# Two attention sweeps of a graph kernel: the leaky slope made by VectorE alone, from a sum in SBUF

## The reference, cut to what matters

```python
xl = (x @ Wl).reshape(n, heads, dh)
xr = (x @ Wr).reshape(n, heads, dh)
m = xl[src] + xr[dst]
e = jnp.einsum('ehd,hd->eh', jax.nn.leaky_relu(m, 0.2), att)
emax = jax.ops.segment_max(e, dst, num_segments=n)
ex = jnp.exp(e - emax[dst])
denom = jax.ops.segment_sum(ex, dst, num_segments=n)
alpha = ex / denom[dst]
out = jax.ops.segment_sum(alpha[..., None] * xl[src], dst, num_segments=n)
```

## Time and profile before

| | |
|---|---|
| median of three runs | 9611.01 us |
| the profiled execution, its own time | 9569.96 us |
| its span, first to last instruction | 9568.0 us |
| busy, share of the span | TensorE 50% (weight loads 44%), VectorE 55%, ScalarE 32%, GpSimd 49% |
| granted TensorE clock, mean | 0.685 of full |
| the 16 DMA engines, mean rate | 157 GB/s |
| from 6370 to 9474 us (the two `gatv2` sweeps with the stage between them) | VectorE busy 1784.5 of 3104.0 us, ScalarE 1025.1, GpSimd 1519.1, DMA share 0.44 |

### The profile page before, as it was taken

The page is one execution under the profiler, slowest core; times in us unless marked ns, Lnnn a source line. Parts: engine busy times, 40 slices in busy tenths (PEclk is TensorE's granted clock), DMA queues, the critical chain, the costliest instruction groups (busy, mean ns, idle before and its releaser), DMA issues. The chain is left out here.

```text
span 9568.0 us, 100223 instructions
## 1 busy us (share of the span) xinstructions
PE 4784.9 (50%) x25909; PEld 4224.4 (44%) x25909; DVE 5255.1 (55%) x9516; ACT 3094.4 (32%) x5510; POOL 4727.2 (49%) x4980
## 2 busy tenths in 40 slices
PE   2667676565555556555544434334444443444443
PEld 2656565455545355454523333333333332433332
DVE  5655555465655456555544444455555554555555
ACT  1555555222222122222222222223333332333332
POOL 4555552454554345544445555544455444454454
PEclk6565557777777777777766666666666666666665
DMA  4666553566666466666646665534444433444443
GB/s 111 173 170 175 167 166 100 170 210 198 204 196 190 141 194 210 191 189 188 187 126 177 178 180 175 173 108 127 130 133 132 125 119 110 130 133 130 129 132 101
DMA packets 1303017, 1502.46 MB, mean 157 GB/s; under 512 B 397380, under 2 KB 994787, under 8 KB 1302452
## 3 DMA queue, kind: packets, MB, share of 16 engines
q1 hardware_dynamic: 1105428, 1005.88, 34.4%
q0 software_dynamic: 197024, 490.18, 18.8%
HBM read 1070.45 MB, written 423.22 MB: 156 GB/s over the span
## 5 line engine op out<-in xcount | busy, mean ns | idle before, releaser
L778 POOL DMA_INDIRECT s_rows<-kv_tab,src_col x2346 | 2223.8, 948 | 2218.0 <-DVE s_msg L1077 1349.3
L923 PE MATMUL bank<-s_msg,s_hot 128*128 128x144 f32 (+1 forms) x9408 | 2076.8, 373 | 1620.8 <-issue 957.1
L923 PEld LDWEIGHTS bank<-s_msg,s_hot 128*128 128x128 f32 x9408 | 1748.0, 258 | 1819.8 <-issue 1098.3
L778 POOL DMA_INDIRECT s_rows<-xl_tab,src_col x1564 | 1479.3, 946 | 1513.5 <-DVE s_msg L1077 980.4
L898 PE MATMUL bank<-s_qwin,s_hot_t 128*128 128x128 f32 (+1 forms) x9408 | 1680.5, 328 | 310.7 <-issue 199.2
L818 ACT ACTIVATE s_part<-bank 128x288 f32<-128x288 f32 (+1 forms) x2352 | 895.5, 401 | 2751.2 <-remote 1590.8
L978 DVE TENSOR_TENSOR_SCAN bank<-s_neg,bank 32x128 f32<-32x128 f32 (+1 forms) x588 | 243.3, 414 | 2749.8 <-remote 2553.5
L898 PEld LDWEIGHTS bank<-s_qwin,s_hot_t 128*128 128x128 f32 x9408 | 1582.2, 252 | 301.6 <-issue 240.2
L778 POOL DMA_INDIRECT s_rows<-gat_tab,src_col x782 | 741.7, 948 | 602.3 <-DVE s_msg L1077 362.3
L812 ACT ACTIVATE s_prob<-s_diff 32x128 f32<-32x128 f32 (+1 forms) x588 | 181.0, 308 | 2517.2 <-DVE s_diff L987 1814.1
L905 PE MATMUL bank<-ident,s_seg_max 32*128 32x32 f32 (+1 forms) x588 | 166.4, 283 | 1514.7 <-ACT s_prob L812 1239.4
(11 more groups left out here) (312 smaller groups left out, 4696.2 us busy)
## 6 DMA issues: line engine op xcount, KB each, us to landing
s_qwin<-q_tab SPq DMA_DIRECT2D x3920, 64.0 KB
part_tab<-s_part SPq DMA_DIRECT2D x294, 576.0 KB
part_tab<-s_part SPq DMA_DIRECT2D x294, 544.0 KB
s_ranks<-rank_tab SPq DMA_DIRECT2D x588, 256.0 KB
s_attr_t<-attr_tab SPq DMA_DIRECT2D x196, 512.0 KB
attr_tab<-s_attr_t SPq DMA_DIRECT2D x98, 512.0 KB
s_rows<-kv_tab,src_col POOLq DMA_INDIRECT x2346
s_rows<-xl_tab,src_col POOLq DMA_INDIRECT x1564
```

The lines of the kernel that those rows point to most:

```text
L778: pool.indirect_dma_start(out=rows[u][:, t, :], out_offset=None, in_=tab, in_offset=bass.IndirectOffsetOnAxis(ap=pl.src_col[:, i * G + t:i ...
L923: ins = pe.matmul(part_ps[c % 2][:, t * W:(t + 1) * W], hot[u][:, PAIR * c + t, :], msg[u % 2][:, PAIR * c + t, :], start=True, stop=True)
```

## The change

In the two `gatv2` sweeps the leaky slope no longer passes through ScalarE. `sums` is gone as a separate step for both halves. For each half VectorE now adds the PSUM bank and the gathered rows into the SBUF tile `prod[h]` and posts `q_used`; then one `scalar_tensor_tensor` reads `prod[h]` twice and writes max(0.2 v, v) back over it; the product with the attention vector and the reduction follow as before. The two ScalarE instructions of each group (L826), their semaphores and the waits on them go. STEPS is 4, as each half has two stepped instructions. All of the first half's chain now stands ahead of the second half's sum.

```diff
-        STEPS = {"gat": 6, "gatv2": 2}.get(kind, 0)
+        STEPS = {"gat": 6, "gatv2": 4}.get(kind, 0)
...
-        if kind == "gatv2":
-            summed, sloped = sem("summed"), sem("sloped")
...
-                def slopes(i, k, u, n, h):
-                    wait(act, summed, 2 * i + h + 1)
-                    if n >= 1:
-                        wait(act, alpha_done, 2 * (i - 1) + h + 1)
-                    act.activation(prod[h][:, :, :], q_ps[h][:, :].rearrange("p (t d) -> p t d", t=HALF), ACT.Copy, scale=0.2
-                                   ).then_inc(sloped, 1)
...
-                    if kind == "gatv2" and has(n):
-                        slopes(*g, 0)
-                        slopes(*g, 1)
...
-                def sums(i, k, u, n):
-                    wait(v, gathered[u], 16 * (G * k + tiles_of(n)))
-                    for h in range(2):
-                        wait(v, q_done, 2 * i + h + 1)
-                        q = q_ps[h][:, :].rearrange("p (t d) -> p t d", t=HALF)
-                        v.tensor_tensor(q, q, rows[u][:, h * HALF:(h + 1) * HALF, :], ALU.add).then_inc(summed, 1)
...
-                    then = stepper(i, h)
+                    then = stepper(i, 2 * h)
...
                     if kind == "gatv2":
-                        wait(v, sloped, 2 * i + h + 1)
-                        v.tensor_tensor(prod[h][:, :, :], q, prod[h][:, :, :], ALU.max).then_inc(q_used, 1)
+                        v.tensor_tensor(prod[h][:, :, :], q, rows[u][:, t0:t1, :], ALU.add).then_inc(q_used, 1)
                         wait(v, q_used, 2 * i + h + 1)
+                        flat = prod[h][:, :, :].rearrange("p t d -> p (t d)")
+                        then(v.scalar_tensor_tensor(flat, flat, 0.2, flat, ALU.mult, ALU.max))
                         then(v.tensor_tensor(prod[h][:, :, :], prod[h][:, :, :], bc(att_ps.unsqueeze(1), [P, HALF, D]),
                                              ALU.mult))
...
-                        if kind == "gatv2" and has(n):
-                            sums(*g)
```

## The result

The changed kernel takes 9314.01 us (median of 4 runs, 9284.96 to 9358.39) against 9608.49 for the kernel before (4 runs, 9577.22 to 9613.73). The ratio is 0.9694, 95% interval [0.9654, 0.9734]: 3.1% faster, some 294 us. The forecast was 9554 with a range of 9460 to 9640.

The account below looks back on a forecast made before the run. Waits were taken to set the time, through a cycle of paired groups of VectorE's first-group path and GpSimd's gathers. Terms -2 - 47 - 8 = -57 us took the median 9611.01 to 9554 us, range 9460 to 9640.

Parts of the forecast that it names:

- ScalarE's relief: ScalarE in the gatv2 sweeps: two instructions fewer per group, 234 us of busy time, costed at nothing for the total.
- The chain's own length: VectorE, first sum to `messages`: 5.52 us against 5.54 before, -2 us over some 98 first groups.
- The order of the halves: VectorE, late second sums: first half's chain runs during the wait; 24 long waits give 47 us, 13 short ones 8.
- The clash of slope and gathers: VectorE's slope with two SBUF operands beside GpSimd's gathers: costs a gather about 0.1 us at worst.
- Rival 2: Second group of a pair: VectorE's slopes block GpSimd's gathers, 1.38 us per pair, 135 us slower, 9689; chance 0.10.
- I take the tie as it is: Stall ahead of L978: TensorE's completions come late while GpSimd gathers; cause unknown from the profile, given no term.
- Rival 3 downwards: Pattern of group pairs shifts: a third of the groups go from 15.0 to 13.6 us, 91 us more gained, 9464; chance 0.10.

Follow-up runs that it names:

- The load put back: Two scaled copies given back to ScalarE: in the changed kernel with the slope's second operand in PSUM, ratio 0.9969; in the whole changed kernel, 0.9778.
- the copies moved first: Kernel before, with ScalarE's first two copies of partial sums moved ahead of its two slopes: 9596.52 us, ratio 0.9979.
- the half-gathers run: Kernel before, gatv2 sweeps with four gathers a group instead of eight, the rest by one plain load of fixed rows: 8400.33 us, ratio 0.8741.
- the fills: Kernel before, gatv2 sweeps with two short GpSimd fills of a spare tile per group: ratio 0.9833; 1.017 when the chip ran it in 6756.02 us.

## Why the prediction was right in sign and wrong in size

That the sign came out right is luck. The term that was to bring the gain, the order, shows no worth; the gain came from ScalarE's relief, which the sum put at nothing, and from the slope's two SBUF operands, which the sum had only as a rival, and as a loss.

- **The chain's own length** was right: slope 0.693 us, first sum to `messages` 8518.59 - 8513.06 = 5.53 us in the excerpt above, for 5.52 forecast. The term of -2 us stands.
- **The order of the halves**, the forecast's -47 and -8 us, failed: with the sums back in front the time is the same (0.9676 against 0.9694). The path behind one late sum is shorter as forecast (6.96 us in the old order, 5.04 in the new, for 1.94 forecast), but nothing of it reached the total. The sum waits did not shrink by a third of 154.6; they tripled, to 468.9 us put down to "remote" in both sweeps, since the stall moved there.
- **ScalarE's relief** "I cost at nothing" failed. The prediction argued that none of ScalarE's effects "is what L978 waits for in the stall". The load put back costs 108 us with whole gathers and 80 with stretched ones; and the copies moved first took the stall from 486.9 to 206.9 us by themselves (255.2 with the waits put down to "issue"). I had judged by the label: the waits name no ScalarE, yet the engines' lists allow the path ScalarE's copies, TensorE's next piece, its completions, VectorE. That it goes this way is argued from the lists, not shown.
- **The clash of slope and gathers** is the step that failed most, in size and in sign: "a clash thus costs a gather about 0.1 us at worst" came from L1058, which has one SBUF operand and so was the wrong row. With two SBUF operands a gather is held up for as much as 0.51 us (1.462 - 0.947). Rival 2 had the mechanism with a price of one sign only. In the cycle with the stall, the clash paid 157 us (184 where ScalarE keeps its load): the stall shrinks, and more of TensorE's completions arrive inside the run. Rival 2 would have been right about the other condition, in kind: 61 us slower, 0.31 us for each of 196 groups, where it had 1.38 us for each of 98 pairs.
- **"I take the tie as it is"**: the prediction saw that TensorE's completions come late while GpSimd gathers, and took the stall's length as given. That tie was the largest item that anything could move. The most that it can be worth lies in the half-gathers run, 1219 us, though that run also drops half of the gathers' own time.
- **Rival 3 downwards** is what the profile shows: full pairs became rarer (idle stretches of over 6 us at the first maximum 37 and 36 before, 4 and 12 after), the period fell to 13.6 and 13.8. Its bound of a third of the groups was too narrow, and it put the cause at ScalarE and TensorE alone.

In one order the parts are: two SBUF operands 157 us, ScalarE's relief 108, and 30 us (0.9969, interval touching 1) not told from none. That they make 295 proves nothing, as each is the step from one kernel to the next. In the other order the same two steps are 80 us for the relief and 184 for the operands, so the sizes hold within some 30 us.

The Trainium skill, SBUF — State Buffer, section "Who interferes with whom", says that a VectorE instruction with two SBUF inputs contends with a GpSimd instruction that reads SBUF, and that one with at most one such input does not, outside the modes that use two ports. The runs agree: no gather is stretched with the slope's second operand in PSUM, and 217 of 1564 are with both in SBUF. The slope itself is hardly ever the one that waits: its median is 0.693 us, its longest 0.759.

**What stays open.** What ties TensorE's completions to an unbroken run of gathers was not found; the half-gathers run and the fills show that it is there, not what it is. Nor was it found how a break acts, as most completions don't arrive in it. Nor was it found what puts the chip in the condition where the tie exists (the kernel before 9542 to 9768 us over all runs) or out of it (6751 to 6773 us). Slower transfers are not it: for the changed kernel the queue of the plain loads and stores was busy 35.2% of 9311.6 us in the one and 47.2% of 6822.3 in the other, 3278 and 3220 us. TensorE's clock is not enough: its busy time differs by 446 us of 2489. Same program, same chip, other hour. So the change's worth is 3.1% in the one and -0.9% in the other, and no kernel of this study beats the kernel before in both. The form that keeps the gathers whole, which would give 1.4% and 0%, was only run with the wrong second operand; the real slope needs its sum twice, and a form of it with one SBUF operand was not tried.

## What to carry to other kernels

When a wait is labelled remote and ends just after another engine's run of work ends, treat that run as part of the cycle, and price everything that touches it (a stretch, a gap, an engine upstream relieved) with both signs instead of at nothing. An interference rule tells that two instructions clash, not who profits: where the engine held up is the bound, the clash costs its length, and where its uninterrupted run goes with a stall of others, the clash may pay. A row used to bound a clash must have the same number of SBUF operands as the new instruction, and a change whose gain comes from a stall is measured again when the stall is gone.

## What the runs showed of the hardware that was not expected

- One 128x512 VectorE instruction with two SBUF operands stretches an indirect gather on GpSimd from 0.947 to at most 1.46 us in the changed kernel, 29 to 41 ns in the mean over 1564 gathers; the VectorE instruction's median does not move.
- In one condition of the chip the semaphore event of TensorE's transpose, and with it the scan that needs it, comes a median of 14.2 us after the transpose in 75 stalls, beside a run of gathers with gaps of 0.30 us; in the other the scan started at most 0.95 us after the transpose in 196 groups, beside the same gathers. Two breaks of 0.33 us in a group of eight gathers take 1.7% off the time of the whole kernel.
- The same kernel on the same chip took 9749 us and, less than an hour later, 6765; the stalls, not the durations of VectorE's and GpSimd's instructions, are the difference: the first maximum lasts 0.41 us and a gather 0.95 in both.
- The granted clock of TensorE was 0.683 in the mean in the changed kernel at 9311.6 us of span and 0.795 at 6822.3, with the same count of matmuls. TensorE stood idle less between its pieces in the second (busy 64% of the span against 52%).
